# Scattering the last experts' results straight to the output: a two-layer decoder with experts on one Trainium2 core

## The chip, the cores and the metric

The kernel runs on one core of a Trainium2 chip. The core has five engines that run their own programs and meet only at semaphores: TensorE (PE, with its weight loads as PEld), VectorE (DVE), ScalarE (ACT), GpSimd (POOL) and SyncE (SP, which here only issues DMAs). The metric is the device time of one execution in microseconds, as the median of the runs shown; less is better.

## The reference, cut to what matters

The whole is a decoder of two layers on x [16, 256, 256]: attention, cross attention and experts, each added to x after a normalisation. The change concerns the last step, the experts of layer 1. In words and cut to that step:

```python
h = layernorm(x)                      # over the last axis, 256 wide, 4096 tokens
logits = h @ gate_w.T + gate_b        # 64 experts
e = argmax(logits)                    # one expert for each token
y = h @ expert_w[e] + expert_b[e]     # expert_w is [64, 256, 256]
result = x + y                        # [16, 256, 256], float32
```

## The kernel before

x stays in SBUF all along as `sh.x` (`x_resident`), 32 tiles of 128 tokens by 256. The last function, `l1_experts` (L3583), works in these stages, each a block that all engines enter and leave together.

**Routing.** `route` gives each token a slot among 6144 sorted rows, so that the tokens of one expert lie together and each group of 32 rows (a segment) has one expert. `slots` holds the slot of each token, `table` the expert of each segment. Meanwhile SP loads all 64 experts' weights (`ew`, 16 MB).

**Sending** (block with L3034, L3637 to L3660). For each of the 32 tiles DVE writes the normalised rows to one of four buffers `xs` (L3025), and POOL sends them with an indirect DMA to their slots in DRAM, `sorted_tokens` (L3034). A buffer is written again when its send has landed (`s_sent`). Beside that PE picks each token's bias row by a product of the turned choice matrix with the biases (L3637, L3646), and DVE adds it to `sh.x` (L3660), two tiles behind.

**Experts** (L3770 and around). 48 tiles of 128 sorted rows, four segments each. SP loads a tile to one of six buffers `xg` (L3701, L3706) as soon as the tile before in that buffer has been turned (`s_tp`). PE turns it (L3720), ACT copies it out (L3747), and the weights of its four segments are copied from `ew` to `w_now`, a ring of three tiles, by three engines in shares: over two tiles DVE copies three segments (L3779), ACT two (L3754), POOL three (L3770). We call such a copy, 128 by 512 numbers, a pick. PE multiplies (L3731), DVE copies the product to `y`, a ring of three (L3790), and SP stores it to its place in `sorted_results` (L3708). `over_tiles` writes out the first and last six tiles and loops over the rest.

**Gathering.** For each of the 32 tiles of tokens POOL fetches the rows of `sorted_results` by `slots` with an indirect DMA (L3811) to one of eight buffers, DVE adds them to `sh.x` (L3819), and SP stores four tiles at a time to the output (L3825).

Long before that, in the first attention, SP fills `sorted_tokens` with zeros (L457), so that slots that no token takes hold numbers.

Of the kernel before, what the change touches and what calls it, by code (L numbers as in the profile page):

```python
# [178 lines left out]
def load_and_prepare(nc, sh, x, ctx_in, early, a0, x0, zeros, ready):  # L179


    with ExitStack() as ctx:
# [17 lines left out]
        with nc.Block() as block:  # L200
# [41 lines left out]
            def _(pool):  # L242
# [5 lines left out]
                pool.memset(zeros[:], 0.0).then_inc(s_const, 1)  # L248
# [80 lines left out]
CLEAR_ROWS = P * 8  # L329
CLEARS = ROWS // CLEAR_ROWS  # L330


class Sorted:
# [74 lines left out]
def l0_attention(nc, sh, early, ready, x0, scratch, zeros, s_cleared):  # L408
# [5 lines left out]
    with ExitStack() as ctx:  # L414
# [34 lines left out]
        with nc.Block() as block:  # L449
            @block.sync  # L450
            def _(sp):
# [3 lines left out]
                for n in range(CLEARS):  # L455
                    dst = scratch.tokens[n * CLEAR_ROWS:(n + 1) * CLEAR_ROWS, :].rearrange("(p r) d -> p (r d)", p=P)
                    sp.dma_start(dst, zeros[:]).then_inc(s_cleared, 16)  # L457
# [2556 lines left out]
def dispatch_programs(nc, sh, sem, top_k, slots, xs, scratch_tokens, sent_before):  # L3014


    s_n, s_sent = sem("dispatch_normalised"), sh.sent

    def vector(dve, between=None):

        for t in range(TILES):
            n = t % BUFFERS
            if t >= BUFFERS:
                dve.wait_ge(s_sent[n], sent_before + 16 * top_k * (t // BUFFERS))
            dve.tensor_scalar(xs[:, n, :], sh.x[:, t, :], sh.stats[:, t, 0:1], sh.rstd[:, t:t + 1], ALU.subtract,  # L3025
                              ALU.mult).then_inc(s_n, 1)
            if between:
                between(t)

    def pool(gp):  # L3030
        for t in range(TILES):
            gp.wait_ge(s_n, t + 1)
            for j in range(top_k):
                gp.indirect_dma_start(scratch_tokens, bass.IndirectOffsetOnAxis(ap=slots[:, j, t:t + 1], axis=0),  # L3034
                                      xs[:, t % BUFFERS, :], None).then_inc(s_sent[t % BUFFERS], 16)
        for n in range(BUFFERS):
            gp.wait_ge(s_sent[n], sent_before + 16 * top_k * TILES // BUFFERS)

    return vector, pool


# [541 lines left out]
def l1_experts(nc, sh, scratch, gate, expert_w, expert_b, result, sent, gathered):  # L3583
# [5 lines left out]
    NT = 48  # L3589
    D, RING = 6, 3  # L3590
    assert NT * PER >= (BATCH * SEQ + E * (SEG - 1)) // SEG
    with ExitStack() as outer:
# [5 lines left out]
        with ExitStack() as ctx:  # L3598
# [12 lines left out]
            with ExitStack() as send:  # L3611
# [4 lines left out]
                xs = sb("xs", [P, BUFFERS, DIM])  # L3616
                pickT = sb("pickT", [E, 2, P])
                c_ps = [ps(f"c_ps{n}", [P, 512]) for n in range(2)]
                b_ps = [ps(f"b_ps{n}", [P, 512]) for n in range(2)]
                s_cp, s_c, s_bp, s_biased = sem("choice_in_psum"), sem("choice_turned"), sem("bias_in_psum"), sem("bias_added")  # L3620
                vector, pool = dispatch_programs(nc, sh, sem, K, slots, xs, scratch.tokens, sent)
                LATE = 2
                with nc.Block() as block:
                    block.gpsimd(pool)
# [6 lines left out]
                    def _(pe):  # L3631
# [8 lines left out]
                        for t in range(TILES):  # L3640
# [16 lines left out]
                    def _(dve):  # L3657
                        def add(t):
                            dve.wait_ge(s_bp, t + 1)
                            dve.tensor_tensor(sh.x[:, t, :], sh.x[:, t, :], b_ps[t % 2][:, 0:DIM], ALU.add).then_inc(s_biased, 1)  # L3660

                        vector(dve, lambda t: add(t - LATE) if t >= LATE else None)
                        for t in range(TILES - LATE, TILES):
                            add(t)
# [240 lines left out]
```

## Time and profile before

| | |
|---|---|
| median of 3 runs | 2865.4 us (2863.39 to 2870.27) |
| the profiled execution's own time | 2872.54 us |
| its span, first to last instruction | 2870.4 us |
| mean granted TensorE clock | 0.928 |
| PE busy | 2516.5 us (88%) |
| DVE busy | 2087.3 us (73%) |
| ACT busy | 1448.5 us (50%) |
| POOL busy | 1062.1 us (37%) |

Busy is the time in which an engine worked at an instruction; it is an average over stages that have different limits. Positions in the trace are microseconds from the span's start. The last function's sending, experts and gathering lie between 2691 and 2870.

### The profile page before, as it was taken

The numbers are of one execution on the slowest core, as the hardware profiler recorded it, in microseconds if no ns is written. First come the engines' busy times: TensorE is split into PE (matmuls) and PEld (weight loads), VectorE is DVE, ScalarE is ACT, GpSimd is POOL, SyncE is SP. The second block draws the span as 40 slices with busy tenths as digits, with TensorE's granted clock in tenths as the row PEclk, the third lists the DMA queues.
The fourth block names the chain that finished last, engine by engine and source line by source line (L and its number), as shares of the span: only waits on it lengthen the run. The fifth ranks groups of instructions, "written<-read, shape, count | busy, mean of one in ns | idle before, by whom it ended". The sixth has DMA issues, their size and how long they took to land. (4 is left out here: it accounts for less than half of the span.)

```text
span 2870.4 us, 59454 instructions
## 1 busy us (share of the span) xinstructions
PE 2516.5 (88%) x19717; PEld 2103.3 (73%) x19717; DVE 2087.3 (73%) x4615; ACT 1448.5 (50%) x3401; POOL 1062.1 (37%) x1584
## 2 busy tenths in 40 slices
PE   6987899999868999999499999999996979996682
PEld 5875788888757999999378888888885946664231
DVE  5884898998647777776488888888865567774664
ACT  3542334334335777777265555656552456673041
POOL 3231545445301111110265555555532014343366
PEclk9988999999978999999699999999998979998586
DMA  8012000000267666664200000000001732220845
GB/s 311 0 32 88 1 1 0 0 0 0 80 243 260 221 220 219 219 220 148 90 14 11 16 7 15 7 15 9 7 1 61 249 102 85 85 83 15 269 142 168
DMA packets 156637, 266.66 MB, mean 93 GB/s; under 512 B 20944, under 2 KB 130464, under 8 KB 143200
## 3 DMA queue, kind: packets, MB, share of 16 engines
q1 hardware_dynamic: 140400, 215.91, 22.1%
q0 software_dynamic: 11168, 31.21, 3.7%
q10 hardware_dynamic: 4944, 17.96, 1.6%
q8 instruction: 67, 1.10, 0.2%
q14 instruction: 58, 0.48, 0.1%
HBM read 191.85 MB, written 73.17 MB: 92 GB/s over the span
## 5 line engine op out<-in xcount | busy, mean ns | idle before, releaser
L1728 ACT ACTIVATE a_prob<-a_s_ps,a_ntop 128x256 f32<-128x256 f32 x512 | 236.1, 474 | 303.8 <-DVE a_ntop L1813 303.8
L1781 POOL TENSOR_TENSOR a_prob<-a_prob,a_rden 128x1024 f32<-128x1024 f32 x128 | 242.8, 1897 | 302.0 <-DVE a_rden L1818 302.0
L3246 POOL DMA_INDIRECT e0x_xg<-token_rows,e_order x78 | 75.3, 965 | 387.2 <-PE e0x_t_ps L3293 342.9
L2416 ACT ACTIVATE x1a_prob<-x1a_st_ps,x1a_mask_now 128x512 f32<-128x512 f32 x256 | 162.4, 686 | 91.5 <-PE x1a_st_ps L2335 90.0
L1306 ACT ACTIVATE x0b_sq<-x0b_f 128x1024 f32<-128x1024 f32 x64 | 67.9, 1061 | 274.2 <-DVE x0b_f L1380 274.1
L2491 DVE TENSOR_REDUCE x1a_top<-x1a_s_ps 128x4 f32<-128x1024 f32 x128 | 154.9, 1222 | 67.1 <-PE x1a_s_ps L2319 65.2
L1813 DVE TENSOR_REDUCE a_ntop<-a_s_ps 128x4 f32<-128x1024 f32 x128 | 156.2, 1220 | 38.7 <-PE a_s_ps L1651 38.5
L68 PE MATMUL e0x_up_ps<-e0x_xT_high,e0x_up_w_high 128*128 128x256 f32 x624 | 180.6, 289 | 1.0 <-DVE e0x_up_w_low L3373 1.0
L68 PE MATMUL e0x_up_ps<-e0x_xT_high,e0x_up_w_low 128*128 128x256 f32 x624 | 177.7, 285 | 0.0
L68 PE MATMUL e0x_up_ps<-e0x_xT_low,e0x_up_w_high 128*128 128x256 f32 x624 | 177.5, 284 | 0.0
L68 PE MATMUL e0x_y_ps<-e0x_down_w_high,e0x_hT_high 128*128 128x256 f32 x624 | 176.6, 283 | 0.0
L68 PE MATMUL e0x_y_ps<-e0x_down_w_low,e0x_hT_high 128*128 128x256 f32 x624 | 176.6, 283 | 0.0
L68 PE MATMUL e0x_y_ps<-e0x_down_w_high,e0x_hT_low 128*128 128x256 f32 x624 | 176.6, 283 | 0.0
L1825 DVE COPY a_pT<-a_pT_ps 128x512 f32<-128x512 f32 x256 | 161.0, 670 | 0.7 <-PE a_pT_ps L1660 0.7
L1660 PE MATMUL a_pT_ps<-ident,a_prob 128*128 128x128 f32 x1024 | 139.9, 279 | 0.0
L1671 PE MATMUL a_o_ps<-a_pT,a_v 128*64 128x256 f32 x1024 | 138.8, 392 | 1.2 <-DVE a_outT_low L1829 1.2
L1840 DVE SCALAR_TENSOR_TENSOR a_kqT_low<-a_fill,a1w_kq_bias,a_kqT_high 128x256 fp32r<-128x256 f32 x256 | 108.9, 477 | 33.1 <-ACT a_kqT_high L1741 33.1
L3387 DVE TENSOR_TENSOR e0x_hT_low<-e0x_h,e0x_hT_high 128x512 fp32r<-128x512 f32 x156 | 104.4, 689 | 37.5 <-ACT e0x_hT_high L3350 37.5
L1179 POOL TENSOR_TENSOR x0b_tree<-x0b_f 128x1024 f32<-128x1024 f32 x32 | 76.4, 2387 | 148.8 <-DVE x0b_f L1380 146.4
L1660 PEld LDWEIGHTS a_pT_ps<-ident,a_prob 128*128 128x128 f32 x1024 | 109.5, 141 | 18.3 <-issue 1.4
L68 PEld LDWEIGHTS e0x_up_ps<-e0x_xT_high,e0x_up_w_high 128*128 128x128 f32 x624 | 120.8, 194 | 1.4 <-issue 1.4
L68 PEld LDWEIGHTS e0x_up_ps<-e0x_xT_low,e0x_up_w_high 128*128 128x128 f32 x624 | 120.7, 193 | 0.0
(648 smaller groups left out, 8714.3 us busy)
## 6 DMA issues: line engine op xcount, KB each, us to landing
e0x_up_raw<-up_rows SPq DMA_DIRECT2D x39, 1024.0 KB, 4.8
e0x_down_raw<-down_rows SPq DMA_DIRECT2D x39, 1024.0 KB
x_qk<-head_rows SPq DMA_DIRECT2D x384, 64.0 KB
head_rows<-x1p_rows_out SPq DMA_DIRECT2D x32, 512.0 KB, 3.8
e1w_ew<-in_L_ffn_expert_w_dram SPq DMA_DIRECT2D x8, 2048.0 KB
sorted_tokens<-zeros SPq DMA_DIRECT2D x10, 1024.0 KB, 19.6
sorted_results<-e0x_y SPq DMA_DIRECT2D x39, 256.0 KB
down_rows<-e0w_downT ACTq DMA_DIRECT2D x8, 1024.0 KB, 6.8
```

What stands on the lines that cost most here:

```text
L68: last = pe.matmul(out, a[x], b[y], start=at == 0, stop=at == n - 1)
L1179: step.then(pool.tensor_tensor(tree[:], src[:, :, 0:HD // 2], src[:, :, HD // 2:HD], ALU.add))
L1660: last = pe.transpose(pT_ps[n][:, j, t * P:(t + 1) * P], prob[:, h % RING, n, t, j * P:(j + 1) * P], sh.ident[:])
L1671: last = pe.matmul(o_ps[h % 2][DH * n:DH * (n + 1), 0:SEQ], v[:, j, at:at + DH], pT[:, h % 2, n, j, :], start=j == 0, stop=j == TPB - 1)
L1728: last = act.activation(prob[:, h % RING, n, t, :], s_ps[:, n, t * SEQ:(t + 1) * SEQ], ACT.Exp, bias=ntop[:, h % RING, n, t:t + 1], accum_ ...
L1781: last = pool.tensor_tensor(p, p, scale_of, ALU.mult)
L1813: dve.tensor_reduce(ntop[:, h % RING], s_ps[:].rearrange("p n (t s) -> p n t s", t=TPB), AXIS.X, ALU.max, negate=True).then_inc(s_top, 1)
L1825: dve.tensor_copy(pT[:, h % 2, n], pT_ps[n][:]).then_inc(s_pT, 1)
L1840: last = dve.scalar_tensor_tensor(kqT[1][:, number, side, :], bank[:, side * SEQ:(side + 1) * SEQ], kq_bias[:, side, number:number + 1], k ...
L2416: last = act.activation(prob[:, c % 2, j, 2 * (h % 2):2 * (h % 2) + 2, :], st_ps[:, :, j * SEQ:(j + 1) * SEQ], ACT.Exp, bias=mask_now[:, p ...
L2491: dve.tensor_reduce(dst, s_ps[h % 2][:].rearrange("p n (t s) -> p n t s", t=TPB), AXIS.X, ALU.max).then_inc(s_max, 1)
L3387: dve.tensor_tensor(part[1], h[:, n, :], part[0], ALU.subtract).then_inc(s_hl, 1)
```

## The change

A row that is sent is now 513 numbers wide: the normalised token, then x plus its bias (which no longer goes back to `sh.x`), then the token's number, as an integer. The experts' tiles load such rows whole. DVE no longer copies the product: it adds the row's second part to it, and POOL scatters the sum with an indirect DMA, by the number in the row, straight to the output. `sorted_results` of this stage, the gathering stage and the last stores are gone. Rows that no token takes hold a number far above any token's (the bits of 1.0), and the scatter skips numbers past its bound.

With that come these edits. A buffer `xg` is loaded again only when the scatter of its tile has landed (`s_st`), since the scatter reads the number from it. The picks are shared out anew over six tiles: DVE 11, ACT 11, POOL 2. POOL's picks run two tiles ahead of its scatters, and POOL's program of the stage is written out for all 48 tiles, with no loop. `w_now` takes the place of `sh.x`. In the sending block the bias product has four PSUM buffers and not two, and a send waits for the bias sum of its own tile. The fill at the start covers 6144 rows of 2052 bytes in 12 DMAs and not 10240 rows of 1024 bytes in 10.

```diff
+SENT_TILES = 48
+SENT_ROWS = SENT_TILES * P
+SENT_WIDTH = 2 * DIM + 1
+CLEAR_ROWS = P * 4
+CLEARS = SENT_ROWS // CLEAR_ROWS
+NO_TOKEN = 1.0
...
-        self.tokens = nc.dram_tensor("sorted_tokens", [ROWS, DIM], F32, kind="Internal").ap()
+        self.tokens = nc.dram_tensor("sorted_tokens", [SENT_ROWS, SENT_WIDTH], F32, kind="Internal").ap()
...
 (sending, PE)
-                            if t >= 2:
-                                pe.wait_ge(s_biased, t - 1)
-                            pe.matmul(b_ps[t % 2][:, 0:DIM], pickT[:, t % 2, :], eb[:], start=True, stop=True).then_inc(s_bp, 1)
+                            if t >= B_RING:
+                                pe.wait_ge(s_biased, t - B_RING + 1)
+                            pe.matmul(b_ps[t % B_RING][:, 0:DIM], pickT[:, t % 2, :], eb[:], start=True, stop=True).then_inc(s_bp, 1)
...
 (sending, DVE)
+                        dve.wait_ge(s_ids, 1)
+                        for t in range(TILES):
+                            n = t % BUFFERS
+                            if t >= BUFFERS:
+                                dve.wait_ge(s_sent[n], sent + 16 * (t // BUFFERS))
+                            dve.tensor_scalar(xs[:, n, 0:DIM], sh.x[:, t, :], sh.stats[:, t, 0:1], sh.rstd[:, t:t + 1], ALU.subtract, ALU.mult)
+                            dve.tensor_copy(xs_token[:, n, 2 * DIM:SENT_WIDTH], ids[:, t:t + 1])
                             dve.wait_ge(s_bp, t + 1)
+                            dve.tensor_tensor(xs[:, n, DIM:2 * DIM], sh.x[:, t, :], b_ps[t % B_RING][:, 0:DIM], ALU.add).then_inc(s_biased, 1)
...
 (sending, POOL)
+                        pool.iota(ids[:], [[P, TILES]], base=0, channel_multiplier=1, allow_small_or_imprecise_dtypes=True).then_inc(s_ids, 1)
+                        for t in range(TILES):
+                            pool.wait_ge(s_biased, t + 1)
+                            pool.indirect_dma_start(scratch.tokens, bass.IndirectOffsetOnAxis(ap=slots[:, 0, t:t + 1], axis=0),
+                                                    xs[:, t % BUFFERS, :], None).then_inc(s_sent[t % BUFFERS], 16)
...
 (experts)
-            SHARES = dict(dve=((0, 1), (0,)), act=((2,), (1,)), pool=((3,), (2, 3)))
+            SHARES = dict(dve=((0, 1), (0, 1), (0, 1), (0,), (0, 1), (0, 1)),
+                          act=((2,), (2, 3), (2, 3), (1, 2), (2, 3), (2, 3)),
+                          pool=((3,), (), (), (3,), (), ()))
...
 (experts, SP)
-                            sp.wait_ge(s_tp, i + 1)
+                            sp.wait_ge(s_st[n % RING], 16 * (D // RING * turn + n // RING + 1))
                             sp.dma_start(xg[:, n, :], scratch.tokens[bass.ds((i + D) * P, P), :]).then_inc(s_ld[n], 16)
-                        sp.wait_ge(s_y, i + 1)
-                        sp.dma_start(scratch.results[bass.ds(i * P, P), :], y[:, n % RING, :]).then_inc(s_st[n % RING], 16)
...
 (experts, POOL)
+                    def tile(i, n, turn):
+                        if not (isinstance(i, int) and i >= NT - 2):
+                            picked(i + 2, (n + 2) % D)
+                        pool.wait_ge(s_y, i + 1)
+                        pool.indirect_dma_start(tokens_out, bass.IndirectOffsetOnAxis(ap=xg_token[:, n, 2 * DIM:SENT_WIDTH], axis=0),
+                                                y[:, n % RING, :], None, bounds_check=P * TILES - 1,
+                                                oob_is_err=False).then_inc(s_st[n % RING], 16)
+
+                    for i in range(NT):
+                        tile(i, i % D, i // D)
...
 (experts, DVE)
-                        dve.tensor_copy(y[:, n % RING, :], y_ps[n % 2][:, 0:DIM]).then_inc(s_y, 1)
+                        dve.tensor_tensor(y[:, n % RING, :], xg[:, n, DIM:2 * DIM], y_ps[n % 2][:, 0:DIM], ALU.add).then_inc(s_y, 1)
...
 (gathering: the whole block removed)
-                        pool.indirect_dma_start(y[:, n, :], None, scratch.results[0:NT * P, :],
-                                                bass.IndirectOffsetOnAxis(ap=slots[:, 0, t:t + 1], axis=0)).then_inc(s_got[n], 16)
...
-                        dve.tensor_tensor(sh.x[:, t, :], sh.x[:, t, :], y[:, n, :], ALU.add).then_inc(s_sum, 1)
...
-                        sp.dma_start(dst[:, t:t + GROUP, :], sh.x[:, t:t + GROUP, :]).then_inc(s_out, 16)
```

## Rows read from the trace of the kernel before

**Rows 1.** The page: the span, and the end of the chain by line.

```profile
span 2870.4 us, 59454 instructions
...
POOL e1c_y L3811 1%; DMA e1c_y<-sorted_results,e_slots 0%; DVE x_resident L3819 0%; POOLq L3803 0%; DVEq L3803 0%; PEldq L3803 0%
```

**Rows 2.** Stages: stretch, length, busy time of engines (instructions), clock, DMA, GB/s.

```profile
2645.00:2691.00 46.00, 14.81 (x30) 6.88 (x30) 30.45 (x58) 0.59 (x1) 0.73 (x4) 0.61 0.90 285
2691.00:2744.00 53.00, 47.75 (x96) 20.12 (x96) 24.18 (x64) 8.24 (x32) 30.95 (x32) 0.50 0.44 150
2744.00:2824.00 80.00, 69.74 (x864) 30.59 (x864) 56.37 (x120) 42.73 (x96) 50.53 (x72) 0.95 0.51 158
2824.00:2871.00 47.00, 0.00 (x0) 0.00 (x0) 13.15 (x32) 0.00 (x0) 30.40 (x32) 0.50 0.59 179
```

**Rows 3.** The chain that ended last, in order of time: start, length, what.

```profile
2824.67 1.01 POOL e1c_y L3811
2825.68 0.30 issue
...
2831.01 3.00 DMA e1c_y<-sorted_results,e_slots
...
2842.28 3.88 DMA e1c_y<-sorted_results,e_slots
...
2866.70 0.34 DVEq L3803
```

**Rows 4.** Groups by line, last stages: busy us, mean ns, idle before, releaser.

```profile
L3770 POOL COPY e1x_w_now<-e1w_ew 128x512 f32 x72 | 50.5, 729 | 29.3 <-PE e1x_y_ps L3731 23.0 <-issue 6.2
L3779 DVE COPY e1x_w_now<-e1w_ew 128x512 f32 x72 | 41.8, 607 | 4.2 <-issue 4.0
...
L3754 ACT COPY e1x_w_now<-e1w_ew 128x512 f32 x48 | 29.9, 623 | 0.0
...
L3747 ACT COPY e1x_xgT<-e1x_t_ps 128x256 f32<-128x256 f32 x48 | 17.9, 373 | 38.0 <-PE e1x_t_ps L3720 38.0
```

**Rows 5.** Timeline of the sending block: start, length, what, idle before.

```profile
2692.38 1.12 POOL L3034 DMA_INDIRECT sorted_tokens<-e1s_xs,e_slots  x1 [40.29 <-DVE e1s_xs L3025]
...
2698.36 0.41 DVE L3025 TENSOR_SCALAR e1s_xs<-x_resident,x_stats,x_rstd 128x256 f32<-128x256 f32 x1 [2.79 <-DMA sorted_tokens<-e1s_xs,e_slots]
...
2734.14 0.41 DVE L3025 TENSOR_SCALAR e1s_xs<-x_resident,x_stats,x_rstd 128x256 f32<-128x256 f32 x1
...
2734.82 0.96 POOL L3034 DMA_INDIRECT sorted_tokens<-e1s_xs,e_slots  x1 [0.41 <-DVE e1s_xs L3025]
...
2743.42 2.72 SPq L3701 DMA_DIRECT2D e1x_xg<-sorted_tokens  x6
```

**Rows 6.** One tile's instructions (`x_resident`): min/median/max ns, first and last start.

```profile
L3660 DVE TENSOR_TENSOR x_resident<-x_resident,e1s_b_ps x32: 402/422/422, 2693.7 to 2740.7; 128x256 f32<-128x256 f32 x32
```

**Rows 7.** The same for the tile `e1x_y`.

```profile
L3790 DVE COPY e1x_y<-e1x_y_ps x48: 405/424/426, 2749.2 to 2820.9; 128x256 f32<-128x256 f32 x48
```

**Rows 8.** Timeline of the experts' stage, a tile in its middle and the last pick.

```profile
2771.49 0.44 PE L3720 MATMUL e1x_t_ps<-ident,e1x_xg 128*128 128x128 f32 x2
...
2771.75 2.12 POOL L3770 COPY e1x_w_now<-e1w_ew 128x512 f32 x3 [0.85 <-PE e1x_y_ps L3731]
...
2772.20 1.20 DVE L3779 COPY e1x_w_now<-e1w_ew 128x512 f32 x2
...
2774.82 0.42 DVE L3790 COPY e1x_y<-e1x_y_ps 128x256 f32<-128x256 f32 x1 [0.67 <-PE e1x_y_ps L3731]
...
2819.10 0.41 DVE L3779 COPY e1x_w_now<-e1w_ew 128x512 f32 x1
```

**Rows 9.** DMA issues, last stages: count, KB each, median us from issue to landing.

```profile
e1x_xg<-sorted_tokens SPq DMA_DIRECT2D x48, 128.0 KB, 2.1
sorted_results<-e1x_y SPq DMA_DIRECT2D x48, 128.0 KB, 1.7
```

**Rows 10.** The fill of `sorted_tokens` in the first attention: durations of the issues, starts.

```profile
L457 SPq DMA_DIRECT2D sorted_tokens<-zeros x10: 432/432/2197, 30.3 to 36.3; - x10
...
DMA to landing us min/median/max: 10.4/19.6/26.7
```

More of the change, by code:

```diff
@@ L176, in __init__, with load_and_prepare @@
         USED.extend([self.s_w, self.s_b])
[L179 removed]
+def load_and_prepare(nc, sh, x, ctx_in, early, a0, x0, unsent, ready):
     with ExitStack() as ctx:
@@ L405, in __init__, with l0_attention @@
         self.qbias = sb("qbias", [P, KC])
-def l0_attention(nc, sh, early, ready, x0, scratch, zeros, s_cleared):
+def l0_attention(nc, sh, early, ready, x0, scratch, unsent, s_cleared):
     with ExitStack() as ctx:
@@ new lines, in _ @@
+                    @block.gpsimd
+                    def _(pool):
+                        pool.iota(ids[:], [[P, TILES]], base=0, channel_multiplier=1, allow_small_or_imprecise_dtypes=True).then_inc(s_ids, 1)
[3 more added lines that the diff above has]
+                                                    xs[:, t % BUFFERS, :], None).then_inc(s_sent[t % BUFFERS], 16)
+                        for n in range(BUFFERS):
+                            pool.wait_ge(s_sent[n], sent + 16 * TILES // BUFFERS)
@@ L3673, in l1_experts, with picked_by_pool @@
             s_ld = [sem(f"tile_loaded{n}") for n in range(D)]
-            s_st = [sem(f"result_stored{n}") for n in range(RING)]
+            s_st = [sem(f"outputs_stored{n}") for n in range(RING)]
             s_tp, s_t, s_yp, s_y = sem("x_turned_in_psum"), sem("x_turned"), sem("y_in_psum"), sem("y_ready")
             s_picked = s_picked_dve, s_picked_act, s_picked_pool = [sem(f"weights_picked_{who}") for who in ("dve", "act", "pool")]
-            SHARES = dict(dve=((0, 1), (0,)), act=((2,), (1,)), pool=((3,), (2, 3)))
+            SHARES = dict(dve=((0, 1), (0, 1), (0, 1), (0,), (0, 1), (0, 1)),
+                          act=((2,), (2, 3), (2, 3), (1, 2), (2, 3), (2, 3)),
+                          pool=((3,), (), (), (3,), (), ()))
+            POOL_PICKS = sum(len(share) for share in SHARES["pool"])
+            def picked_by_pool(n, turn):
+                return POOL_PICKS * turn + sum(len(share) for share in SHARES["pool"][0:n + 1])
             def copies(engine, who, i, n):
-                segments = SHARES[who][n % 2]
+                segments = SHARES[who][n]
                 experts = [engine.value_load(table[0:1, bass.ds(i * PER + g, 1)], min_val=0, max_val=E - 1) for g in segments]
@@ L3721, in turn_x, with product @@
                         last.then_inc(s_tp, 1)
-                    def product(i, n):
-                        for picked in s_picked:
-                            pe.wait_ge(picked, i + 1)
+                    def product(i, n, turn):
+                        pe.wait_ge(s_picked_dve, i + 1)
+                        pe.wait_ge(s_picked_act, i + 1)
+                        pe.wait_ge(s_picked_pool, picked_by_pool(n, turn))
                         pe.wait_ge(s_t, i + 1)
@@ L3737, in tile @@
                             turn_x(i + 1, (n + 1) % D, turn + (1 if n == D - 1 else 0))
-                        product(i, n)
+                        product(i, n, turn)
                     turn_x(0, 0, 0)
@@ L3765, in _, with picked @@
                 def _(pool):
-                    def tile(i, n, turn):
-                        pairs = copies(pool, "pool", i, n)
-                        wait_past(pool, s_yp, i - RING + 1)
-                        for pair in pairs:
-                            last = pool.tensor_copy(*pair)
-                        last.then_inc(s_picked_pool, 1)
-                    over_tiles(pool, tile)
+                    def picked(i, n):
+                        for pair in copies(pool, "pool", i, n):
+                            wait_past(pool, s_yp, i - RING + 1)
+                            pool.tensor_copy(*pair).then_inc(s_picked_pool, 1)
+                    for i in range(2):
+                        picked(i, i)
+                    def tile(i, n, turn):
+                        if not (isinstance(i, int) and i >= NT - 2):
[6 more added lines that the diff above has]
+                        tile(i, i % D, i // D)
+                    for n in range(RING):
+                        pool.wait_ge(s_st[n], 16 * NT // RING)
                 @block.vector
```

87 lines of the change are left out of this document (18 added, 69 removed).

## The prediction

> **What bounds the kernel now.** Start with the page: one core, a span of 2870.4 us, and a chain that ends in the gathering stage, on POOL's indirect DMAs [rows 1]. Then cut the last 180 us into stages, because the busy shares of the whole span say nothing about them [rows 2]. Each has its own limit.
>
> In the gathering stage (2824 to 2871) PE and ACT do nothing. The chain alternates a gather's issue of 0.95 to 1.01 us with 0.30 us of gap [rows 3]: 32 gathers at 1.25 us are 40 us, and the rest is the first wait, some waits for landings and the last store. Nothing overlaps this stage, so what goes with it goes from the end.
>
> In the sending block PE is busy 47.75 of 53 us, at a granted clock of 0.50, which is the 1.2 GHz level [rows 2]. The bias additions run from 2693.7 to 2740.7 [rows 6], 31 steps of 1.52 us. So PE's bias product sets this pace, not POOL, whose sends take 0.96 + 0.30 = 1.26 us.
>
> In the experts' stage the 48 products are taken out from 2749.2 to 2820.9 [rows 7], 47 steps of 1.526 us. PE is busy 69.74 us, 1.45 us a tile [rows 2]: it is nearly the limit, with short waits for picks between.
>
> **What is removed.** The gathering stage. What stays behind the last tile's product is its sum on DVE (0.42 us), the hand-over to POOL, the scatter and the end of the block. The hand-over is read from a send: DVE wrote `xs` until 2734.14 + 0.41 = 2734.55, the send began at 2734.82, so 0.27 us [rows 5]. The scatter itself is not in this trace. Its nearest row is the gather of the same 128 rows of 1 KB: 3.00 to 3.88 us from the start of the issue to landing [rows 3]. I take 3.0, since a plain store of this size lands sooner than a plain load (1.7 against 2.1 us [rows 9]). With 0.5 us for the block's end, the span ends 0.42 + 0.27 + 3.0 + 0.5 = 4.2 us after the last sum begins. Before, it ended 2870.4 - 2820.9 = 49.5 us after that point. Removed: 45.3 us.
>
> **What the sending block gains.** Before, the last send left some 3 us before the last bias addition; now it comes after it. The last addition ends at 2740.7 + 0.42 = 2741.1, and the next block's first load was issued at 2743.42 [rows 5], 2.3 us later. Now 0.27 us of hand-over and a landing of 3.0 us come between: +3.3 us. Bounds: the gather's 3.88 and the doubled bytes give +4.5; PE freed of its early stalls gives back up to 0.8.
>
> Does the send, twice as wide, set the pace? A buffer `xs` goes round in 0.41 (normalise) + some 0.15 (the number, estimated as well under the 0.42 of a full addition) + 0.42 (bias sum) + 0.27 + 3.0 to 3.9 (send) = 4.3 to 5.2 us, and four buffers at PE's 1.52 us leave 6.1. No. While the weights are still loading a send lands late, 2698.36 - 2692.38 = 5.98 us [rows 5], in the stretch after one of 0.90 DMA share [rows 2]. A round is then over 7 us, some 1 us too long for two rounds. Four PSUM buffers let PE run ahead meanwhile, and POOL catches up at 1.26 us against 1.52. I put 0. The new iota and wait lie before the first bias product; they are covered by it.
>
> **What the experts' stage becomes.** Five rings must be held against the old 1.526 us a tile:
>
> - PE: unchanged, 1.45.
> - ACT: the turn's copy 0.373 + 11/6 picks of 0.623 [rows 4] = 1.52.
> - DVE: the sum 0.42 + 11/6 picks. A pick is 0.41 alone and 0.607 in the mean beside POOL's picks [rows 4, 8]: 1.17 to 1.53.
> - POOL: 1.25 for the scatter + 1/3 of a pick of 0.729 [rows 4] = 1.49.
> - The buffer `xg`, new: it is loaded only after its scatter. From the start of the sum: 0.42 + 0.27 + 3.0 to 3.88 (scatter), 0.1 for SP, the load of 2.1 us [rows 9] + 0.4 for the second 128 KB at about the 285 GB/s that the weights got [rows 2], and from the turn of a tile to its sum 2774.82 - 2771.49 = 3.33 us [rows 8] (the turn is issued before the previous tile's product, so one tile period is in it). Sum 9.6 to 10.5 us for six tiles: 1.60 to 1.75.
>
> The ring `y`, three tiles, needs (0.42 + 0.27 + 3.0 + 0.1)/3 = 1.26 and is slack. So the `xg` ring comes last, and four engines stand at 1.45 to 1.53 right behind it, which leaves no slack to absorb irregularity. To this comes the neighbour on POOL's side: POOL's three picks took 2.12 us beside two picks of DVE, which took 1.20 [rows 8], where DVE's alone take 0.41. Both engines lengthen when they work at once, by 0.1 to 0.2 us a pick. The scatter will run beside DVE's two picks, because both are released by the same sum. I add half such a step to the ring's middle and take 1.68 us: 47 x (1.68 - 1.526) = +7.2 us. Bounds: 1.49, if nothing is lost and the landing is quick (-1.7), and the port case below. The first loads of the stage carry twice the bytes: +0.3.
>
> **Costed at nothing.** The fill of 12 DMAs, 12.6 against 10.5 MB: the issues begin at 30.3 and landed after 10 to 27 us, behind which nothing on SP waits but the block's end [rows 10]; uncovered it would be some 5 us. The sum of two operands against the copy of one: 0.42 both ways [rows 6, 7]. POOL's program without a loop: the 32 gathers were written out too and kept 0.30 us gaps [rows 3].
>
> **The sum.** -45.3 + 3.3 + 0.3 + 7.2 = -34.5 us. The profiled execution took 2872.5, so it would take 2838.0; the median of the runs is 2865.4, 7.1 lower, and the same step from it gives 2830.9 us.
>
> **Rivals.**
>
> *Nothing is lost between the engines.* The stage stays at 1.49 to 1.55: -1.7 to +1.1 instead of +7.2, so 2822 to 2825. For it: the engines' own sums. Against it: the `xg` ring is 1.60 even with the quickest landing. Chance 0.18.
>
> *POOL and DVE exclude one another.* A pick of 512 numbers out of SBUF takes DVE 0.41 us, no more than the 0.42 for 256 numbers out of PSUM [rows 7, 8], so it runs at twice the pace and may need a path that POOL uses too. If a pick and the writing of a scatter's descriptors can't overlap at all, a tile needs 0.95 (issue) + 11/6 x 0.41 + 1/3 x 0.62 = 1.91 us, or with a hand-over of 0.27 between them 2.18: +18 to +31 us, so 2842 to 2855. For it: the lengthened picks above. Against it: those picks overlapped in part, 2.12 and 1.20 us side by side. No indirect DMA of the old trace lies beside such a copy. Chance 0.22.
>
> The Trainium skill states the rule in SBUF — State Buffer, "SBUF: two separate sides": a VectorE copy of fp32 within SBUF shuts GpSimd out of the port pair that both share, so it can't write the descriptors of its DMAs. By that rule the exclusive case holds; this trace's picks beside picks lengthen by far less than a whole instruction each, and no row here shows it for descriptors.
>
> *The scatter lands late.* The three buffers of `y` wait for landings. With a landing of L us this ring gives (0.79 + L)/3 a tile, from L = 5 on more than the `xg` ring, and L counts once more behind the sending block and once at the end: -41.7 + 2 (L - 3) + 47 x ((0.79 + L)/3 - 1.526) = -107 + 17.7 L us. At L = 6.1 the gain is gone, above 6.5 the kernel is slower by over 0.3%. A send beside the weights took 5.98 us, where the DMA engines were nearly full; the experts' stage has them at 0.51 [rows 2, 5], and the loads double while the stored rows shrink by a third, say 0.68. At 5.98 the time is 2864. Chance 0.08, of which 0.05 slower.
>
> *The change doesn't save the stage.* Some skipped row or check makes each scatter so long (2.4 us a tile on POOL) that the experts' stage takes back what the gathering gave: no change. POOL's issue varied only from 0.95 to 1.12 us over reads and writes [rows 3, 5]. Chance 0.04.
>
> **Chances and range.** The forecast has 0.48. The range must reach to the quick case and well into the exclusive one: 2820 to 2850; the forecast's own is 2825 to 2839. A change of 0.3%, 8.6 us, is about what can be told from none. Faster: the forecast, the quick and the exclusive case and a part of the late one, 0.90. Same 0.04, slower 0.06.
>
> **What would show it.** No L3811 after the experts' stage. The last bias sum near 2740 and the first load of the experts near 2746.7. Sums (the old L3790) at 1.68 us, with PE's turns waiting for loads of `xg`; if POOL's scatter is 1.5 us or more instead of 0.96 and DVE's picks beside it lengthen, the exclusive case is right; if DVE waits for landings before its sums, the late one. The prediction is wrong if the scatter's issue or landing is far from the gather's, or if the wide send holds up PE.

## The result and the profile after

The changed kernel takes 2852.4 us in the median of 17 runs (2843.9 to 2862.4); in the same session the kernel before took 2868.3 (17 runs, 2860.9 to 2874.0). The ratio is 0.9952, with a 95% interval of 0.994 to 0.9963: a gain of some 14 us. Forecast were 34.5 us of gain and 2830.9 us, with a range of 2820 to 2850. The sign was right and the size was not; the time lies above the range.

The profiled execution took 2862.39 us, 10 above the median. Its last function started at 2695.9, where that of the eleven variants below starts between 2684.4 and 2692.6, in code that is the same but for the fill at the start. So the absolute positions are not compared; all that follows is counted from the first turn of the choice matrix (the start of the sending block's PE work), 2691.7 before and 2695.9 after.

The page of the changed kernel, its span and the end of its chain:

```profile
span 2860.5 us, 59335 instructions
...
DMA out_dram<-e1x_y,e1x_xg 1%; DMA e1x_xg<-sorted_tokens 1%; PE e1x_y_ps L3726 0%; DVEq L3681 0%; DVE x_resident L3786 0%; PE e1x_t_ps L3714 0%; DVE e1x_y L3797 0%; POOL out_dram L3773 0%; POOL x_resident L3764 0%; DVEq L3786 0%; ACT x_resident L3749 0%; SPq L3704 0%; POOLq L3681 0%; DVEq L3688 0%; DVEq L49 0%
```

Stages of the changed kernel, with the columns of [rows 2]: sending to the last send, the passage to the first load, the passage to the first sum, the sums, and what follows the last one's start:

```profile
2695.90:2745.40 49.50, 47.68 (x96) 20.10 (x96) 25.93 (x96) 8.21 (x32) 30.36 (x32) 0.50 0.68 232
2745.40:2754.00 8.60, 0.00 (x0) 0.00 (x0) 0.00 (x0) 0.00 (x0) 0.96 (x1) 0.50 0.16 61
2754.00:2760.40 6.40, 3.35 (x21) 1.36 (x22) 1.52 (x4) 2.30 (x5) 0.61 (x1) 0.50 0.78 248
2760.40:2852.80 92.40, 71.60 (x844) 31.37 (x844) 53.96 (x132) 61.15 (x131) 56.14 (x62) 0.95 0.57 166
2852.80:2860.50 7.70, 0.00 (x0) 0.00 (x0) 0.38 (x1) 0.00 (x0) 1.50 (x2) 0.69 0.01 0
```

The gathering's lines are gone from the chain. In their place stand scatters and loads of the experts' tiles, and below them L3681, the line on which an engine reads an expert's number from the table into a register. The second view says where the forecast failed: 48 sums in 92.4 us with PE busy 71.6. The same stretch of the kernel before, from its first to its last copy of a product [rows 7], with two products of the changed kernel's experts' stage under it:

```profile
2749.20:2820.90 71.70, 66.63 (x844) 29.25 (x844) 54.56 (x116) 41.04 (x92) 47.86 (x68) 0.98 0.52 160
```

```profile
2785.62 1.92 PE L3726 MATMUL e1x_y_ps<-x_resident,e1x_xgT 128*32 128x256 f32 x16
...
2791.07 1.07 PE L3726 MATMUL e1x_y_ps<-x_resident,e1x_xgT 128*32 128x256 f32 x16
```

So PE's holes grew from 71.7 - 66.6 = 5.1 us to 92.4 - 71.6 = 20.8 us, and its busy time grew by 5.0 us for the same 844 matmuls. The granted clock tells the second part: 0.98 before, 0.95 after. In the first tiles both kernels run at the 1.2 GHz level. The changed one falls back to it twice more: behind PE's wait of 1.61 us for a load, up to 2782.82 (granted clock 0.58 from 2784 to 2788) and behind one of 1.76 us, up to 2807.43 (0.59 from 2808 to 2812). A product takes 1.92 or 1.94 us there instead of 1.07. A wait of 1.88 us before 2771.05 brought no such fall; what decides it isn't shown.

The instructions of the tile `e1x_y` in the changed kernel:

```profile
L3797 DVE TENSOR_TENSOR e1x_y<-e1x_xg,e1x_y_ps x48: 420/421/423, 2760.4 to 2852.8; 128x256 f32<-128x256 f32 x48
L3773 POOL DMA_INDIRECT out_dram<-e1x_y,e1x_xg x48: 966/974/1222, 2761.7 to 2854.0; - x48
```

So 47 steps of 1.966 us instead of 1.526, and not the 1.68 of the forecast. Both instructions last about what was put down for them, 0.42 and 0.97 us. From the first sum to the first scatter, though, it is 2761.7 - 2760.4 = 1.3 us, of which the sum is 0.42.

| us | before | after | difference | forecast |
|---|---|---|---|---|
| first turn to first sum | 57.5 | 64.5 | +7.0 | +3.6 |
| first to last sum | 71.7 | 92.4 | +20.7 | +7.2 |
| after the last sum's start | 49.5 | 7.7 | -41.8 | -45.3 |
| together | 178.7 | 164.6 | -14.1 | -34.5 |

The last function alone gives the 14 us of the runs. Of the missing 20.4 us, 13.5 are in the experts' stage, 3.4 before it and 3.5 behind it.

The chain of the changed kernel in the experts' stage, in order of time:

```profile
2762.92 0.43 DVE e1x_y L3797
...
2763.40 0.75 issue
2764.15 0.91 POOL out_dram L3773
2765.05 0.73 issue
2765.79 3.71 DMA out_dram<-e1x_y,e1x_xg
2769.50 0.02 issue
2769.51 3.30 DMA e1x_xg<-sorted_tokens
...
2790.43 0.33 DVEq L3681
2790.79 0.19 DVEq L3681
2791.19 0.08 DVE e1x_y L3797
...
2791.54 0.56 DVE x_resident L3786 x2
```

Two patterns take turns in it. One is the `xg` ring of the forecast: sum, scatter, landing, load. Six times between 2764 and 2850 the chain goes through a scatter's landing, of 3.71, 4.47, 3.66, 3.35, 3.28 and 3.03 us from the start of its issue (mean 3.58), and each time on through a load of 2.62 to 3.30 (mean 2.98). Behind a sum it shows 0.75 us of "issue" before the scatter, where the forecast had 0.27 us of hand-over. The other pattern is DVE's own turn: two reads of the table, the sum, two picks, and again. Waits of the experts' stage, changed kernel (engine, line, what it waited for: total us, times, longest):

```profile
DVE e1x_y L3797 <- PE e1x_y_ps L3726: 32.9, 34, 2.6
...
PEld e1x_t_ps L3714 <- DMA e1x_xg<-sorted_tokens: 24.3, 29, 1.8
PE e1x_t_ps L3714 <- DMA e1x_xg<-sorted_tokens: 16.5, 21, 1.9
...
DVE e1x_y L3797 <- DMA out_dram<-e1x_y,e1x_xg: 3.4, 4, 1.1
```

PE waits for loads of `xg`, as forecast; DVE hardly waits for landings, so the ring `y` is not first.

### The profile page after: what moved, and what is told of

It is laid out like the page before. It is cut to its first block and busy times, and to the rows that moved or that the text cites. A ratio compares the mean times of both kernels' runs of the same rounds, so it can differ in the third digit from the quotient of the medians.

```text
span 2860.5 us, 59335 instructions
## 1 busy us (share of the span) xinstructions
PE 2536.0 (89%) x19717; PEld 2112.9 (74%) x19717; DVE 2075.7 (73%) x4631; ACT 1467.7 (51%) x3441; POOL 1037.5 (36%) x1544
```

## The experiments

In the table every run is divided in the same way as above; "pace" is the time between first and last sum over 47. The run's time is the median where there are several, else the one run.

| | run | to last send | to first load | to first sum | pace | after last sum's start | together |
|---|---|---|---|---|---|---|---|
| before | 2868.3 | 46.1 | 5.6 | 5.8 | 1.526 | 49.5 | 178.7 |
| after | 2852.4 | 49.5 | 8.6 | 6.4 | 1.966 | 7.7 | 164.6 |
| e1_ring12 | 2844.0 | 53.0 | 7.6 | 6.5 | 1.781 | 7.8 | 158.6 |
| e2_no_dve_picks | 2858.1 | 54.4 | 8.1 | 6.5 | 1.849 | 7.8 | 163.7 |
| e6_no_bound | 2853.0 | 53.2 | 8.2 | 6.5 | 1.917 | 7.6 | 165.6 |
| e12_register_bound | 2852.7 | 51.0 | 7.8 | 6.4 | 1.977 | 7.8 | 165.9 |
| e5_number_apart | 2849.7 | 54.7 | 7.9 | 6.5 | 1.832 | 7.7 | 162.9 |
| e8_both_rings | 2846.0 | 54.0 | 8.1 | 6.6 | 1.785 | 7.7 | 160.3 |
| e10_fixed_experts | 2840.4 | 51.9 | 8.4 | 6.4 | 1.626 | 7.7 | 150.8 |
| e3_rows_2304 | 2852.7 | 48.9 | 6.0 | 6.5 | 2.049 | 7.8 | 165.5 |
| e4_sp_waits | 2852.7 | 53.4 | 6.4 | 6.5 | 1.926 | 6.4 | 163.2 |
| e9_all | 2840.0 | 48.9 | 4.4 | 6.5 | 1.783 | 6.4 | 150.0 |
| e11_shares | 2835.2 | 49.0 | 4.4 | 6.9 | 1.662 | 6.5 | 144.9 |

The sending block, whose code is the same in after, e1, e2, e5, e6, e8, e10 and e12, varies from 49.5 to 54.7 us. The experts' stage runs the same code in after and e4, and in e12 but for the bound's register, and the pace is 1.966, 1.926 and 1.977: a difference of 0.05 between two paces, each from one profile, shows nothing. The kernel before took 2862.7 to 2864.6 us in the median beside the variants, and 2868.3 beside the change, so single runs' times are only a frame.

**A longer `xg` ring.** Is it the ring that holds PE?

```diff
-    D, RING = 6, 3
+    D, RING = 12, 3
+            SHARES = {who: shares * 2 for who, shares in SHARES.items()}
```

> Twelve buffers xg in place of six, nothing else. If the ring of xg (sum, hand-over, scatter's landing, load, turn) sets the pace of 1.97 us a tile, twelve buffers halve what it needs and the sums come at 1.6 to 1.75 us, which is POOL's own 0.97 + 0.3 to 0.65 + 0.23: the time falls by 10 to 17 us. If the engines hinder each other (VectorE's picks and GpSimd's scatters excluding one another, 1.91 us a tile or more by the prediction), the pace stays at 1.9 to 2.0 and the time within 3 us.

Measured: 2844.0 us (4 runs), ratio to before 0.992 (0.9896 to 0.9945), pace 1.781. Waits of the experts' stage in this kernel:

```profile
DVE e1x_y L3798 <- DMA out_dram<-e1x_y,e1x_xg: 18.0, 22, 1.6
...
PE e1x_y_ps L3727 <- DVE x_resident L3787: 14.5, 22, 1.2
```

PE's waits for loads are gone from the list, and 0.185 x 47 = 8.7 us with them. PE is busy for 66.9 us between the first and the last sum, at a granted clock of 1.00, so 4.7 of the 8.7 us are the lower clock that the waits had brought. The pace ends just above the 1.6 to 1.75 expected. With twelve buffers `over_tiles` also writes out 24 tiles and not 12; e5, below, comes near this pace without that. What comes next are the ring `y` (DVE waits for landings 22 times) and DVE's picks (PE waits for them 22 times).

**No picks on DVE.** Is it DVE's work beside the scatter's? DVE's copies of weights are left out here, so that their segments are multiplied with whatever lies in `w_now`; DVE only adds.

```diff
-                        pe.wait_ge(s_picked_dve, i + 1)
...
-                        if ahead:
-                            picked(pairs)
```

> VectorE's 88 picks are left out (so the products of those segments use other numbers); the waits for it go too. If VectorE's copies hold off the scatter's start, the time from the end of the sum to the start of the scatter falls from 0.73 to 0.80 us to 0.27, and the pace by 0.1 us a tile or more. If not, it stays at 0.73 to 0.80 and the pace at 1.9 to 2.0.

Measured: pace 1.849 although DVE does nothing but the sum, and the hand-over is unchanged (0.79 to 0.81 us in 39 of 48 tiles). The expectation had tied the two together; the pace fell by 0.08 to 0.12 without the hand-over. Timeline of this kernel, one tile (POOL and DVE):

```profile
2790.95 0.42 DVE L3793 TENSOR_TENSOR e1x_y<-e1x_xg,e1x_y_ps 128x256 f32<-128x256 f32 x1 [1.38 <-PE e1x_y_ps L3725]
2792.16 0.97 POOL L3772 DMA_INDIRECT out_dram<-e1x_y,e1x_xg  x1 [0.82 <-DVE e1x_y L3793]
```

2792.16 - 2791.37 = 0.79 us, with no pick near. So the delay is not DVE's picks. With DVE out of the way the chain between 2765 and 2835 is 31.4% scatters' landings and 30.8% loads: the `xg` ring nearly alone gives 1.85 a tile, at a granted clock of 0.97.

**No bound.** Is it the check of the numbers? The scatter goes to scratch in DRAM instead of the output, without `bounds_check`; rows that no token takes hold numbers behind the tokens', and are written too. The output is not written.

```diff
+                pool.iota(unsent[:]..., [[1, CLEAR_ROWS // P], [0, 1]], base=P * TILES, channel_multiplier=CLEAR_ROWS // P).then_inc(s_const, 1)
...
-            tokens_out = result.rearrange("b s d -> (b s) d")
+            tokens_out = scratch.results[0:P * TILES + CLEAR_ROWS, :]
...
-                                                y[:, n % RING, :], None, bounds_check=P * TILES - 1,
-                                                oob_is_err=False).then_inc(s_st[n % RING], 16)
+                                                y[:, n % RING, :], None).then_inc(s_st[n % RING], 16)
```

> The scatters go without a bound to a buffer in DRAM that has a row for each number, and the rows of no token carry numbers of their own: nothing is skipped, 6144 rows are written and not 4096, and the output is not written. If the bound's set-up makes the hand-over long, it falls from 0.73 to 0.80 us to 0.27 to 0.30; the ring of xg then gives 1.97 - 0.08 = 1.89 us a tile, unless the added rows land later. If the hand-over is the port's doing it stays.

Timeline of this kernel, one tile, and behind it one of the changed kernel:

```profile
2785.42 0.42 DVE L3798 TENSOR_TENSOR e1x_y<-e1x_xg,e1x_y_ps 128x256 f32<-128x256 f32 x1 [0.75 <-PE e1x_y_ps L3728]
2785.76 0.82 DVE L3787 COPY x_resident<-e1w_ew 128x512 f32 x2
...
2786.11 0.96 POOL L3775 DMA_INDIRECT sorted_results<-e1x_y,e1x_xg  x1 [0.94 <-DVE e1x_y L3798]
```

```profile
2791.19 0.42 DVE L3797 TENSOR_TENSOR e1x_y<-e1x_xg,e1x_y_ps 128x256 f32<-128x256 f32 x1 [0.77 <-PE e1x_y_ps L3726]
...
2791.53 0.76 DVE L3786 COPY x_resident<-e1w_ew 128x512 f32 x2
...
2792.41 0.97 POOL L3773 DMA_INDIRECT out_dram<-e1x_y,e1x_xg  x1 [0.88 <-DVE e1x_y L3797]
```

Without the bound the hand-over is 2786.11 - 2785.84 = 0.27 us, with it 2792.41 - 2791.61 = 0.80. Over all tiles: with the bound 37 of 48 lie at 0.79 to 0.81 us, the rest above; without it 36 of 48 at 0.27 or 0.28. The bound costs 0.52 us each time that POOL is ready and only waits for the sum. When POOL is behind and goes from a scatter straight to the next, the gap is 0.30 to 0.31 us with the bound as without it. Pace 1.917, where 0.52/6 = 0.09 a tile was to be had: it is 0.05 below after but only 0.01 below e4, so the hand-over is shown and its worth in the pace is not. Here all 6144 rows are written and none is skipped.

The fence of the unbounded kernel also bears on the rival of the shared port. The scatter's issue (2786.11 to 2787.07) lies beside DVE's two picks (2785.76 to 2786.58) for 0.47 us; it took 0.96, the two picks 0.82 instead of 0.76. Elsewhere two picks beside nothing but a scatter take up to 1.04 us (e1), and in other places the scatter's issue lengthens instead, to 1.22 us at most. So they hinder one another, but not for an instruction's whole length: in the changed kernel all picks beside scatters alone are 1.5 us longer together, 0.03 us a tile, and all issues together 0.8 us. The Trainium skill says in SBUF — State Buffer, "SBUF: two separate sides", that such a copy takes the shared port pair for its whole length and shuts GpSimd out; the rows show a hold of at most 0.28 us on two picks or on a scatter's issue.

**The bound in a register.** Does the cost lie in how the bound is handed over?

```diff
+                    pool.memset(bound[:], P * TILES - 1).then_inc(s_bound, 1)
+                    limit = pool.value_load(bound[0:1, 0:1], min_val=P * TILES - 1, max_val=P * TILES - 1)
...
-                                                y[:, n % RING, :], None, bounds_check=P * TILES - 1,
+                                                y[:, n % RING, :], None, bounds_check=limit,
```

> The changed kernel with one edit: the bound of the scatters comes from a register that is set once before the first tile, and not from a constant. If the 0.5 us between the sum and the scatter is the setting of that register after the wait, the hand-over falls from 0.80 to 0.28 us, the ring of xg by 0.52/6, the pace from 1.93 to 1.97 to 1.85 to 1.88 us a tile, and the last tile ends 0.5 us sooner. If a bounded scatter takes longer in itself, it stays 0.80.

Measured: hand-over 0.79 to 0.81 again in 36 of 48 tiles, pace 1.977. No.

**The number apart.** DVE copies the row's number to a small tile of its own; `xg` is then free after the sum, and its next load doesn't wait for the scatter.

```diff
-                            sp.wait_ge(s_st[n % RING], 16 * (D // RING * turn + n // RING + 1))
+                            sp.wait_ge(s_y, i + 1)
+                        dve.tensor_copy(row_token[:, n % RING:n % RING + 1], xg_token[:, n, 2 * DIM:SENT_WIDTH])
```

> VectorE copies each row's number to a small tile of its own beside the sum, so that a buffer xg is loaded again after the sum and not after the scatter; still six buffers xg and three of y. If the scatter inside the ring of xg sets the pace, this does as much as twelve buffers did: 1.78 us a tile, VectorE waiting for the scatters' landings before some 20 of its sums. If the number of buffers in flight helped in another way, the pace stays above 1.85.

Measured: pace 1.832. Expected was e1's 1.78, and the 0.05 between them is no more than unchanged code shows. The `xg` ring is gone here as in e1, the chain goes through scatters' landings (26.9% between 2765 and 2835) into DVE's wait for a buffer of `y`, 17 times.

**Both rings.** As before, and six buffers of `y` with six semaphores.

```diff
+            Y_RING = 6
+            y = sb("y", [P, Y_RING, DIM])
+                        wait_past(dve, s_st[n % Y_RING], 16 * (D // Y_RING * turn + n // Y_RING))
```

> As the run before, and six buffers of y in place of three. If the ring of y was what came next, the pace is now that of the engines: GpSimd's 0.97 + 0.30 + 0.23 = 1.50 to ScalarE's 1.52, with irregularity 1.55 to 1.65 us a tile, and the time is 6 to 10 us below that with twelve buffers of xg and three of y. If GpSimd's set-up of the bound (0.5 us) counts on every tile, the pace is 0.97 + 0.80 + 0.23 = 2.0 however many buffers there are.

Measured: 2846.0 us (7 runs), ratio 0.9933 (0.9911 to 0.9956), pace 1.785. No engine waits for a landing any more, and the pace stays that of e1. Neither branch of the expectation came true, 1.55 to 1.65 or 2.0: something else held the stage. DVE's timeline in this kernel, with the scatter beside it:

```profile
2792.29 0.15 DVE L3799 COPY e1x_row_token<-e1x_xg 128x1 uint32<-128x1 uint32 x1 [0.90 <-PE e1x_y_ps L3728]
...
2792.36 0.41 DVE L3800 TENSOR_TENSOR e1x_y<-e1x_xg,e1x_y_ps 128x256 f32<-128x256 f32 x1
...
2792.48 0.99 POOL L3775 DMA_INDIRECT out_dram<-e1x_y,e1x_row_token  x1 [0.17 <-issue]
2792.69 1.01 DVE L3788 COPY x_resident<-e1w_ew 128x512 f32 x2
...
2794.13 0.15 DVE L3799 COPY e1x_row_token<-e1x_xg 128x1 uint32<-128x1 uint32 x1 [0.42 <-issue]
```

From one tile to the next DVE needs 2794.13 - 2792.29 = 1.84 us; busy are 0.48 for number and sum and 1.01 for the picks, and then it is idle for 0.42 before the next tile. 0.25 of the 1.01 is the scatter beside them; in the mean over the tiles that is 0.03 us. 1.83 to 1.84 is the commonest step, and six tiles mostly take 10.8 to 11.4 us. What fills the gap the chain says: from 2786 to 2792 its share by line is 42.6% DVE's queue at the line of the table reads and 26.1% its picks. PE waits for DVE's picks 18 times, 12.4 us in all, from the first sums to the last.

**Fixed experts.** As the last, but DVE copies the weights of fixed experts, without reading the table. The result is that of wrong experts in DVE's segments.

```diff
+                if who == "dve":
+                    return [(w_now[:, n % RING, g]..., ew[:, 7 * n + g:7 * n + g + 1]...)
+                            for g in segments]
```

> As the run with both rings freed (1.785 us a tile), but VectorE's picks copy from fixed experts, so it reads no register from the table; the copies themselves are all made (the products of those segments use other experts' weights). If VectorE's reads of the table are what fills its turn of 1.83 us on tiles with two picks (0.42 + 0.15 + 0.76 leave some 0.5), the pace falls to 1.5 to 1.65, where ScalarE and GpSimd stand. If the copies or the shared port bound it, it stays above 1.72.

Measured: pace 1.626. Waits of the experts' stage in this kernel:

```profile
DVE e1x_row_token L3802 <- PE e1x_y_ps L3731: 17.0, 34, 1.3
...
PE e1x_y_ps L3731 <- DVE x_resident L3791: 1.3, 3, 0.4
```

PE hardly waits for DVE's picks (1.3 us instead of 12.4), and DVE waits for PE in 34 of 48 tiles instead of 18. The reads, with the addresses made from them, cost 1.785 - 1.626 = 0.159 us a tile, 7.5 us in the stage, though DVE's copies are no shorter (519 ns in the mean against 470).

**Rows of 2304 bytes.** Do rows of 2052 bytes cost the transfers more than their bytes?

```diff
-SENT_WIDTH = 2 * DIM + 1
+SENT_WIDTH = 2 * DIM + 64
+                        pool.memset(xs[:], 0.0).then_inc(s_ids, 1)
```

> Rows of 2304 bytes (nine times 256) in place of 2052, so 12% more bytes, each row starting on a multiple of 256. If the odd length costs, the fill at the start goes back from some 275 GB/s to over 350, the loads of a tile land in 2.6 us or less and not 3.0, the sends in 3.8 or less and not 4.3, and the pace falls by 0.1 us or more. If only the bytes count, all of them get longer by up to 12%: loads 3.1, pace 2.0.

The sends of `xs`, changed kernel first, then this one (who waited how long and how often, then landings):

```profile
  DMA sorted_tokens<-e1s_xs,e_slots: 19.5, 24
...
DMA to landing us min/median/max: 3.3/4.3/8.4
```

```profile
  DMA sorted_tokens<-e1s_xs,e_slots: 4.7, 5
...
DMA to landing us min/median/max: 2.8/2.8/6.4
```

And the fill at the start, GB/s in 40 slices of the first 100 us, again the changed kernel first:

```profile
GB/s 36 277 356 348 334 299 308 349 348 346 349 349 326 380 380 433 309 233 266 286 305 292 318 263 246 276 286 253 276 276 230 276 164 13 0 0 0 0 0 0
...
sorted_tokens<-unsent SPq DMA_DIRECT2D x12, 1026.0 KB, 30.0
```

```profile
GB/s 31 276 359 349 335 298 310 348 349 346 350 348 348 374 418 427 438 417 420 428 439 420 420 439 424 428 417 413 33 0 7 0 3 0 0 0 0 0 0 0
...
sorted_tokens<-unsent SPq DMA_DIRECT2D x12, 1152.0 KB, 23.6
```

More bytes, less time: the fill runs at 417 to 439 GB/s instead of 230 to 318, a send lands in 2.8 us instead of 4.3, and the sending block takes 48.9 us instead of 49.5 to 54.7. In the end it gives nothing here: the tiles' loads were left whole, 288 KB each, and the pace is 2.049, not the 0.1 us less that was expected. The loads themselves land in 3.1 us in the median against 3.0, which is too little to make that pace, so its cause is open. Whether it is the rows' length or where they start that costs is not separated either.

**SP waits at the end of the blocks.** The waits for the last sends and the last scatters go from POOL's program to SP's.

```diff
+                        for n in range(BUFFERS):
+                            sp.wait_ge(s_sent[n], sent + 16 * TILES // BUFFERS)
...
-                        for n in range(BUFFERS):
-                            pool.wait_ge(s_sent[n], sent + 16 * TILES // BUFFERS)
...
```

> The last waits for the sends and for the scatters are moved from GpSimd to SyncE, which has nothing else to do then. If GpSimd's way out of a block is slow once it waits last, the first load of the experts comes 1 us or more sooner after the last send than the 8.5 us of the changed kernel (from the start of that send), and the span ends 1 us or more sooner after the last sum than 7.7 us. If it is only the landing that is waited for, both stay within 0.5 us.

The last send and the first load in this kernel:

```profile
2741.04 0.96 POOL L3652 DMA_INDIRECT sorted_tokens<-e1s_xs,e_slots  x1 [0.91 <-DVE e1s_xs L3645]
2747.38 2.72 SPq L3699 DMA_DIRECT2D e1x_xg<-sorted_tokens  x6
```

6.34 us between them where the kernels with POOL's wait and the same rows have 7.6 to 8.6, and 6.4 us behind the last sum's start instead of 7.6 to 7.8. So at the last end a landing that POOL waits for costs about 1.3 us more than the same landing seen by SP; at the first the difference is 1.3 to 2.3 us, with landings that vary. The pace, 1.926, is that of unchanged code. In the kernel before POOL waits for the last landing too, and its first load comes 5.6 us after the last send; whether its block ended with that or with the last bias sum no run shows.

**All of it.** The number apart, six `y`, SP's waits, rows of 2304 bytes of which a load takes only the 2052 used.

> The number apart, six buffers of y, the last waits on SyncE, and rows that lie 2304 bytes apart, of which the experts load only the first 2052. If these are four causes, they add up: sending 3 to 7 us shorter (a send lands in 2.8 and not 4.3 to 5.2 us), the pace 1.55 to 1.65 us a tile, the ends 1 to 3 us sooner; some 20 to 30 us below the changed kernel, 2822 to 2832. If the gathering stage's gain is bounded by something else, it stays above 2838.

Measured: 2840.0 us (6 runs), ratio 0.9908 (0.9884 to 0.9932), above the 2822 to 2832 expected, because the pace is not the 1.55 to 1.65 expected. The stage before the first sum is 59.8 us, near the 57.5 of before, the end 6.4, the pace 1.783 as in e8: DVE.

**New shares.** The same with the picks at DVE 9, ACT 12, POOL 3 of 24 instead of 11, 11, 2.

```diff
+            SHARES = dict(dve=((0, 1), (0,)) * 3,
+                          act=((2, 3), (1, 2)) * 3,
+                          pool=((), (3,)) * 3)
```

> The run with all four edits, and the picks shared anew over two tiles: VectorE 9 of 24 in place of 11, ScalarE 12, GpSimd 3. If VectorE's turn (1.83 us with two picks, 1.3 with one) sets the pace of 1.783, it falls to (1.83 + 1.3)/2 = 1.57 to 1.65 us, and the time by 6 to 10 us, to 2830 to 2834. If not, GpSimd with its third pick becomes the limit (1.27 + 0.33, and 0.5 for each bound that it sets late): 1.75 to 1.85, no change.

Measured: 2835.2 us (6 runs), ratio 0.9888 (0.9869 to 0.9907), pace 1.662: the first branch of the expectation, missed by 0.01 us in the pace and by 1 us in the time. It is the fastest version: 29 us faster than before by its own comparison (2864.3), about twice the gain of the change as made. DVE has the share of picks that it had before (1.5 a tile), and DVE and ACT are in the chain beside PE.

## Why the prediction failed where it did

**Right:** the gathering stage is gone whole; the ring `xg` holds PE, with waits of PE for its loads; the sum lasts 0.42, the scatter's issue 0.97; the number's copy 0.147 (forecast 0.15); the scatter's landing, 3.03 to 4.47 in the chain, starts where the gather's 3.00 to 3.88 does. In the changed kernel's profile the bias sums take 46.8 us from the first to the last (2697.9 to 2744.7) against 47.0 [rows 6]. The fill, put at nothing, lands in 30.0 us in the median where it was 19.6 [rows 10]; that the last function starts at 2684.4 to 2692.6 in the variants, against 2691.7 before, shows no loss from it.

**The step that failed: "From the start of the sum: 0.42 + 0.27 + 3.0 to 3.88", the hand-over, and the load of 2.5 behind it.** The hand-over was read from a send, which has no bound; the scatter has one, and the bound makes it 0.80 (e6 against after). With the 0.80, the mean landing 3.58, some 0.1 for SP, the mean load 2.98 (forecast 2.5) and the turn-to-sum time of the forecast, 0.42 + 0.80 + 3.58 + 0.1 + 2.98 + 3.33 = 11.2 us for six tiles, 1.87 a tile. e2, in which this ring is nearly alone, has 1.849. The 3.33 holds a tile's period of before; counted without it, over five tiles and with the 1.51 us from a turn to its sum that the chain shows where nothing lies between (2772.86 to 2774.37), it is 9.39/5 = 1.88. Forecast were 1.60 to 1.75. Against the forecast's shortest sum of 9.6 us the landing gives 0.58, the hand-over 0.53 and the load 0.48. The landing was within its bounds; the hand-over (0.27) and the load (2.5) had none and were both too small.

**The second step: DVE's ring at 1.17 to 1.53.** It summed instructions and left out what DVE's queue does between them. Each pick needs an expert's number read from the table first, and the reads aren't hidden: in the chain above they are 0.33 and 0.19 us, 2790.43 to 2791.19 with what lies between, before the sum. DVE's step is 1.84 and the mean pace 1.785 (e8). Before, DVE had 1.5 picks a tile, and PE waited for them for 5.0 us in all in the experts' stage, so this cost was there and hardly to be seen; the changed shares (11 of 24) uncovered it. e10 takes the reads away and reaches 1.626, e11 takes the picks away and reaches 1.662.

**A third term, at nothing: PE's clock.** PE was put down as "unchanged, 1.45". Its waits for loads brought the 1.2 GHz level back twice, and it was busy 5.0 us longer, 0.11 us a tile. In the variants without these waits it isn't: 66.9 us in e1 and 67.3 in e8, at 1.00 and 0.99.

The three together make up the pace. The sum of what was missed is (1.966 - 1.68) x 47 = 13.4 us: 8.7 go when the ring is longer (e1, 1.781), 4.7 of them as PE's busy time, and the other 4.7 stay with DVE. The ring nearly alone gives 1.85 and DVE 1.785; in one kernel they give 1.926 to 1.977. The clock is 0.8 to 1.7 us of this difference, since PE is busy 69.9 us in e2 and 70.7 to 71.6 us in e4, e12 and after. The rest fits the chain, which goes from one ring to the other, but no run shows that neither makes good what the other lost. The forecast says that it adds half a step of 0.1 to 0.2 us to the ring's middle; the middle of 1.60 and 1.75 is already 1.675, so its 1.68 left nothing for irregularity.

**The passage between the blocks, +3.3.** From the end of the last bias sum to the first load it is 8.8 us, not 5.6. The landing was put at the gather's quickest, 3.0; it is 4.3 in the median and 4.7 to 5.2 in the runs with the same rows, since rows of 2052 bytes go slowly (e3: 2.8). And POOL, which waits for it, takes some 1.3 us to leave (e4); the 2.3 us of before, read as the way from the last bias sum to the first load, may have held that already. With both cured (e9) it is 5.1 us from the last bias sum's end. "I put 0" for the sending itself held in the changed kernel's profile, though DVE waits for landings 24 times there, 19.5 us; in the runs with the same rows the block is 1.5 to 5.2 us longer still. The rows of 2052 bytes were the cause: with 2304-byte rows it is 5 times, 4.7 us, and a block of 48.9 us.

**The end, 4.2 us.** It is 7.7: 0.5 more for the hand-over, 1.3 for POOL as the one that waits, and the rest of 1.7 between the landing, up to 0.6 over the 3.0, and the block's end, for which 0.5 was too little.

**Rivals.** "Nothing is lost" and "the scatter lands late" fell with the pace and with DVE's 4 waits for landings. "POOL and DVE exclude one another" had priced 1.91 to 2.18 us a tile and 2842 to 2855 us, and the result lies in it, with 1.966 and 2852.4; but for another cause. Its own sign, issues of 1.5 us or more, isn't there (0.966 to 1.222 us, median 0.974); picks beside scatters do lengthen, by 0.03 us a tile where the rival's lower case is 0.38 over the old pace. And the 0.80 us before a scatter stays without DVE's picks (e2) and goes without the bound, with the picks in place (e6).

**What stays open.** Why a bounded scatter takes 0.52 us longer to start after a wait, and 0 longer behind another one: only that it hangs on the bound and not on where the bound's value stands. Why the loads in the chain take 2.98 us, 0.48 over the estimate: what row length does was measured on sends and the fill, and for the loads it is open, since e9's, narrow parts of long rows, land in 3.5 us. And what holds e11 at 1.662 over PE's 1.45: its waits are spread over ACT's picks (6.2 us), POOL's and DVE's sums.

## What to carry to other kernels

Cost an engine's turn from the distance between its instructions in the trace, not from the sum of their lengths: register reads before a dynamic copy, and the start of an indirect DMA with a bound, lie in the gaps. When a buffer is made to wait for a store as well as its reader, its ring gets the store's landing on top; copying the few bytes that the store needs elsewhere (0.15 us) takes it out again. When a row is widened by one element, look at what its length does to the transfers before counting bytes.

## What the runs showed of the hardware

- An indirect scatter with a bounds check starts 0.80 us after the instruction it waits for, without one 0.27 to 0.28; issued straight behind another the gap is 0.30 to 0.31 for both. Its issue is 0.97 against 0.96 us.
- Rows of 2052 bytes against 2304: the fill of DRAM at 230 to 318 against 417 to 439 GB/s, an indirect send's landing 4.3 to 5.2 against 2.8 us in the median.
- A block's end that hangs on a DMA's landing is about 1.3 us later when POOL waits for it than when SP does.
- Two reads of numbers from SBUF into registers of DVE take 0.52 us of its queue (0.76 with what lies between) and aren't hidden behind its copies.
- A scatter's issue on POOL and fp32 copies within SBUF on DVE run side by side and hinder one another a little: two copies take 0.75 to 1.04 us beside a scatter and 0.75 to 0.76 alone, the issue up to 1.22 us and mostly 0.97.
- PE's granted clock fell to 0.58 and 0.59 in two stretches of 4 us behind waits of 1.61 and 1.76 us, and a product of 16 matmuls took 1.92 to 1.94 us there, 1.07 elsewhere.
